# Eight images of an attention-and-convolution layer: four image pairs run as one stream of row bands

## The reference, cut to what matters

```python
stk = _neighborhood(x)                      # [B,H,W,9,C], zero padded
q = einsum('bhwd,de->bhwe', x, Q_P)
k = einsum('bhwkd,de->bhwke', stk, K_P)
v = einsum('bhwkd,de->bhwke', stk, V_P)
alpha = softmax(einsum('bhwke,bhwe->bhwk', k, q) * mask, axis=-1)
t = x + einsum('bhwk,bhwke->bhwe', alpha, v)
t_in = t
t = relu(conv(t, ff1_kernel, ff1_bias))     # 64 -> 64 channels
t = relu(conv(t, ff2_kernel, ff2_bias))     # 64 -> 128
t = relu(conv(t, ff3_kernel, ff3_bias))     # 128 -> 64
return t_in + t
```

## Time and profile before

| | |
|---|---|
| median of 3 runs | 2274.04 us (2273.7 to 2277.18) |
| profiled execution, first to last instruction | 2273.2 us; the trace gives no other time of its own for it |
| mean granted clock of PE | 0.992 of full speed |
| PE busy | 2184.7 us, 96% |
| DVE busy | 1889.0 us, 83% |
| ACT busy | 1133.5 us, 50% |
| share of PE in the chain that ended last | 88% |
| DMA | 328.30 MB, mean 144 GB/s |

### The profile page before, as it was taken

The page is one execution under the profiler, slowest core; times in us unless marked ns, Lnnn a source line. Parts: engine busy times, 40 slices in busy tenths (PEclk is TensorE's granted clock), DMA queues, the critical chain, the costliest instruction groups (busy, mean ns, idle before and its releaser), DMA issues.

```text
span 2273.2 us, 64013 instructions
## 1 busy us (share of the span) xinstructions
PE 2184.7 (96%) x24401; PEld 1227.1 (54%) x24401; DVE 1889.0 (83%) x2850; ACT 1133.5 (50%) x3108; POOL 15.5 (1%) x24
## 2 busy tenths in 40 slices
PE   4999999999899999999989999999998999999998
PEld 2655555555455555555555555555545555555554
DVE  4788888888588888888858888888876888888886
ACT  2554555455355555455435555554535555545542
POOL 2000000000000000000000000000000000000000
PEclk9999999999999999999999999999999999999999
DMA  5445544544255445444535454445443544454453
GB/s 131 135 136 159 155 144 132 172 145 143 96 165 155 145 132 171 145 144 142 162 104 152 133 171 145 144 142 165 144 140 103 169 146 142 142 166 144 135 158 124
DMA packets 291252, 328.30 MB, mean 144 GB/s; under 512 B 89300, under 2 KB 223252, under 8 KB 284564
## 3 DMA queue, kind: packets, MB, share of 16 engines
q1 hardware_dynamic: 291164, 327.17, 47.8%
HBM read 152.50 MB, written 33.82 MB: 82 GB/s over the span
## 4 chain that ended last, share of the span: by engine, by line
PE 88%; DVE 6%; issue 3%; ACT 1%; DMA 1%; SPq 1%; DVEq 0%; ACTq 0%
PE conv_banks L485 30%; PE conv_banks L501 25%; PE conv_banks L443 17%; PE mix_bank L421 6%; PE score_banks L394 4%; DVE work L868 3%; PE score_banks L406 3%; PE mix_bank L433 3%; PE score_banks L386 1%; DMA work<-w 1%; ACT probt L646 0%; DVE prob L767 0%; PE mix_bank L370 0%; ACT prob L629 0%; DVE negmax L758 0%
## 5 line engine op out<-in xcount | busy, mean ns | idle before, releaser
L485 PE MATMUL conv_banks<-dodd,w3f 128*64 128x512 f32 (+1 forms) x1656 | 501.9, 580 | 10.8 <-DVE work L835 8.6
L485 PE MATMUL conv_banks<-deven,w3f 128*64 128x512 f32 (+1 forms) x1656 | 495.6, 569 | 8.7 <-DVE prob L767 7.0
L629 ACT ACTIVATE prob<-score_banks,negmax 128x100 f32<-128x100 f32 x1040 | 343.2, 342 | 189.3 <-DVE negmax L758 189.3
L443 PE MATMUL conv_banks<-dt,w1f 128*64 128x256 f32 (+3 forms) x4224 | 413.5, 383 | 12.3 <-DVE work L868 5.6
L501 PE MATMUL conv_banks<-duh,w2h 64*128 64x512 f32 (+2 forms) x1632 | 327.8, 399 | 3.7 <-DVE work L859 2.6
L443 PEld LDWEIGHTS conv_banks<-dt,w1f 128*64 128x64 f32 (+1 forms) x4224 | 218.9, 135 | 206.2 <-issue 69.5
L501 PE MATMUL conv_banks<-duh,w2l 64*128 64x512 f32 (+2 forms) x1632 | 318.5, 388 | 2.1 <-DVE prob L767 2.1
L501 PE MATMUL conv_banks<-dul,w2h 64*128 64x512 f32 (+2 forms) x1632 | 282.6, 397 | 0.0
L485 PEld LDWEIGHTS conv_banks<-dodd,w3f 128*64 128x64 f32 x1656 | 138.6, 137 | 236.8 <-issue 213.2
L646 ACT COPY probt<-score_banks 100x1024 f32<-100x1024 f32 x130 | 131.7, 1013 | 235.1 <-PE score_banks L406 235.1
L485 PEld LDWEIGHTS conv_banks<-deven,w3f 128*64 128x64 f32 x1656 | 155.6, 138 | 157.2 <-issue 111.4
(11 more groups left out here) (93 smaller groups left out, 2943.7 us busy)
## 6 DMA issues: line engine op xcount, KB each, us to landing
xk<-x_keys SPq DMA_DIRECT2D x66, 800.0 KB
xc<-x_bands SPq DMA_DIRECT2D x66, 650.0 KB, 4.9
dodd<-dodd SPq DMA_DIRECT2D x68, 512.0 KB, 5.1
xr<-x_bands SPq DMA_DIRECT2D x264, 128.0 KB, 3.3
out<-work SPq DMA_DIRECT2D x60, 512.0 KB, 2.6
dt<-dt SPq DMA_DIRECT2D x68, 256.0 KB, 2.3
deven<-deven SPq DMA_DIRECT2D x68, 256.0 KB, 5.5
duh<-duh SPq DMA_DIRECT2D x68, 256.0 KB, 2.4
```

The lines of the kernel that those rows point to most:

```text
L443: mm = nc.tensor.matmul(bank[(LOWER, UPPER)[o], n * 256 + lo * 64:n * 256 + hi * 64], w1f[i][rows, m, s, o * C:o * C + C], dt[rows, lo + s ...
L485: return nc.tensor.matmul(bank[rows, lo * 128:hi * 128], w3f[:, m, s, odd * C:odd * C + C], source[:, lo + s // 2:hi + s // 2, m], start=s ...
L629: last = nc.scalar.activation(prob[:, g % 2, a], score_banks[:, g % 2, a * KEYS:(a + 1) * KEYS], ACT.Exp, bias=negmax[:, g % 2, a:a + 1], ...
```

## The change

The four pairs become one stream of 64 bands. The draining step after each of the first three pairs is gone: the next pair's step 0 is now a whole step in every convolution, and it finishes the old pair's last slot of convolutions 1 and 2 and four slots of convolution 3. Step 1 does four slots of convolution 3 too: two of the old pair and two of the new one. There is one draining step at the end (`DRAIN`) and the same final piece (`LAST`, `FINAL`).

Rows of one pair must not reach into the other. So at k = 0 the half-row taps of convolution 1 start at slot 1, and two taps of convolution 2 are cut at the border: one becomes two matmuls of 1 and 2 slots, one runs over 3 slots in place of 4. At k = 1 two of the six taps of each convolution 3 tile are cut in two matmuls (2 and 1 slots, and 1 and 2). The order of two taps in `conv3_tile` and of the two slots in `begin2` is turned, so that the first matmul on a bank covers all of it.

The order of loops changes: step 0 of the first pair stands ahead of the loop; the loop has three turns of step 1, the inner loop, and the next pair's step 0; the last pair's step 1 and inner loop stand behind it, and then the draining step. `store` has no work in the first step; at k = 1 it writes two pieces of two slots to two places. ACT's copies of zeros and the separate regions at k = 0 go; POOL sets four more buffers to zero at the start.

```diff
 def pairs1(k):
-    return (0, 1) if k == BANDS else (0, RP)
+    return (0, 1) if k == DRAIN else (0, RP)
 def pairs2(k):
-    return (1, RP) if k == 0 else (0, 1) if k == BANDS else (0, RP)
+    return (0, 1) if k == DRAIN else (0, RP)
 def pairs3(k):
-    return (2, RP) if k == 1 else (0, 2) if k == 0 else (0, RP)
+    return (0, 2) if k == LAST else (0, RP)
...
         def schedule(eng, step):
-            with eng.Fori(0, PAIRS) as p:
-                g0, b0 = p * STEPS, p * BANDS
-                step(g0, 0, b0 + 1, 1, True)
-                step(g0 + 1, 1, b0 + 2, 0, True)
+            def pair(p):
+                g0 = p * BANDS
+                step(g0 + 1, p, 1, g0 + 2, 0, True)
                 with eng.Fori(0, (BANDS - 2) // 2) as h:
                     for j in range(2):
-                        step(g0 + h * 2 + (2 + j), 2 + j, b0 + h * 2 + (3 + j), 1 - j, True)
-                step(g0 + BANDS, BANDS, b0 + BANDS, 0, False)
+                        step(g0 + h * 2 + (2 + j), p, 2 + j, g0 + h * 2 + (3 + j), 1 - j, True)
+
+            step(0, None, 0, 1, 1, True)
+            with eng.Fori(0, PAIRS - 1) as p:
+                pair(p)
+                step(p * BANDS + BANDS, p, 0, p * BANDS + (BANDS + 1), 1, True)
+            pair(PAIRS - 1)
+            step(RUN, PAIRS - 1, DRAIN, RUN, 0, False)
...
+            def store(G, p, k):
                 lo, hi = pairs3(k)
                 sp.wait_ge(out_ready, G + 1)
-                sp.dma_start(out[:, G, lo:hi], sums[CONV3][:, lo:hi]).then_inc(sent, 16)
+                first = (G + p) * RP
+                if k == 1:
+                    to = slots[:, bass.ds(first - RP, 12)].rearrange("c (n s) i w -> c n s i w", s=6)[:, :, 0:2]
+                    sp.dma_start(to, sums[CONV3].rearrange("c (n s) i w -> c n s i w", n=2)).then_inc(sent, 16)
+                else:
+                    sp.dma_start(slots[:, bass.ds(first, hi - lo)], sums[CONV3][:, lo:hi]).then_inc(sent, 16)
...
             def tap1(k, i, m, n, rows, o, s, start, stop):
                 lo, hi = pairs1(k)
-                if k == 0 and s == 0:
+                if k == 0 and rows is not FULL:
                     lo = 1
...
                     for i, rows, o in ((0, LOWER, 0), (0, UPPER, 1), (1, UPPER, 0), (1, LOWER, 1)):
-                        if o == 0 and k == 0:
-                            tap1(k, i, m, n, FULL, o, 0, False, n == 1)
-                        elif o == 1 or k < BANDS:
-                            tap1(k, i, m, n, rows, o, 1 - o, n == 0 and k == BANDS, n == 1)
+                        if o == 1 or k != DRAIN:
+                            tap1(k, i, m, n, rows, o, 1 - o, n == 0 and k == DRAIN, n == 1)
...
                 def tap(odd, s, start, stop):
                     rows, source = (LOWER, UPPER)[odd], (dodd, deven)[s % 2]
-                    return nc.tensor.matmul(bank[rows, lo * 128:hi * 128], w3f[:, m, s, odd * C:odd * C + C],
-                                            source[:, lo + s // 2:hi + s // 2, m], start=start, stop=stop)
+                    spans = [(lo, hi)]
+                    if k == 1 and s in (0, 3):
+                        spans = [(0, 2), (3, RP)] if s == 0 else [(0, 1), (2, RP)]
+                    for lo_, hi_ in spans:
+                        mm = nc.tensor.matmul(bank[rows, lo_ * 128:hi_ * 128], w3f[:, m, s, odd * C:odd * C + C],
+                                              source[:, lo_ + s // 2:hi_ + s // 2, m], start=start,
+                                              stop=stop and hi_ == hi)
+                    return mm
...
             def tap2(k, which, j, rows, s, w, d, start, stop):
                 lo, hi = pairs2(k)
+                spans = [(lo, hi)]
+                if k == 0 and (which, rows) == (EVEN, LOWER) and s == 0:
+                    spans = [(0, 1), (2, RP)]
+                if k == 0 and (which, rows) == (ODD, UPPER) and s == 1:
+                    spans = [(1, RP)]
...
-            with pe.Fori(0, PAIRS) as p:
-                g0, b0 = p * STEPS, p * BANDS
-                step(g0, 0, b0 + 1, True)
-                step(g0 + 1, 1, b0 + 2, True)
+            def pair(g0):
+                step(g0 + 1, 1, g0 + 2, True)
                 with pe.Fori(0, BANDS - 2) as h:
-                    step(g0 + h + 2, 2, b0 + h + 3, True)
-                step(g0 + BANDS, BANDS, b0 + BANDS, False)
+                    step(g0 + h + 2, 2, g0 + h + 3, True)
+
+            step(0, 0, 1, True)
+            with pe.Fori(0, PAIRS - 1) as p:
+                pair(p * BANDS)
+                step(p * BANDS + BANDS, 0, p * BANDS + (BANDS + 1), True)
+            pair(RUN - BANDS)
+            step(RUN, DRAIN, RUN, False)
...
+            nc.gpsimd.memset(kept[:, 0], 0.0)
             nc.gpsimd.memset(kept[:, 1, 0:2], 0.0)
+            for t in (dt[:, 0:1], duh[:, 0:1].bitcast(F32), dul[:, 0:1].bitcast(F32)):
+                nc.gpsimd.memset(t, 0.0)
```

More of the change, by code:

```diff
@@ L30 @@
 LOADS = PAIRS * BANDS + 3
+RUN = PAIRS * BANDS
+FINAL = RUN + 1
+DRAIN, LAST = BANDS, BANDS + 1
 NEG = -3.0e38
@@ L70, in new_slots @@
 def new_slots(which, k):
-    return {CONV1: 1, ODD: 1, EVEN: 2}[which] if k == BANDS else RP
+    return {CONV1: 1, ODD: 1, EVEN: 2}[which] if k == DRAIN else RP
 def build(nc, x_bands, x_keys, qt2, kt, vbd, w1, w2, w3, b1, b2, b3, window, eye, eye16, out):
@@ L310, in _, with step @@
             keep_first(1, 0)
-            def store(G, k):
+            slots = out.rearrange("c g s i w -> c (g s) i w")
+            def store(G, p, k):
                 lo, hi = pairs3(k)
                 sp.wait_ge(out_ready, G + 1)
-                sp.dma_start(out[:, G, lo:hi], sums[CONV3][:, lo:hi]).then_inc(sent, 16)
-            def step(G, k, b, par, att):
+                first = (G + p) * RP
[4 more added lines that the diff above has]
+                    sp.dma_start(slots[:, bass.ds(first, hi - lo)], sums[CONV3][:, lo:hi]).then_inc(sent, 16)
+            def step(G, p, k, b, par, att):
                 sp.wait_ge(conv1_done, G * 8 + 8)
@@ L326, in step @@
                 sp.dma_start(deven[:, 0:1], deven[:, RP:RP + 1]).then_inc(v_kept, 16)
-                store(G, k)
+                if p is not None:
+                    store(G, p, k)
                 if att:
@@ L341, in _ @@
             schedule(sp, step)
[L342 to L348, removed]
+            store(FINAL, PAIRS - 1, LAST)
+            sp.wait_ge(sent, 16 * (FINAL + 2))
+            sp.wait_ge(t_kept, 16 * (FINAL + 1))
+            sp.wait_ge(u_kept, 32 * (FINAL + 1))
+            sp.wait_ge(v_kept, 32 * FINAL)
+            sp.wait_ge(carried, 48 * (1 + 2 * RUN))
             sp.wait_ge(xk_in, 16 * (LOADS - 1))
@@ L500, in tap2 @@
                 lo, hi = pairs2(k)
-                return nc.tensor.matmul(conv_banks[:, bank_of(which, j), lo * 128:hi * 128],
-                                        w[rows, STREAMS[j], 2 * (which == EVEN) + s],
-                                        d[rows, lo + s:hi + s, STREAMS[j]], start=start, stop=stop)
+                spans = [(lo, hi)]
[3 more added lines that the diff above has]
+                    spans = [(1, RP)]
+                for lo, hi in spans:
+                    mm = nc.tensor.matmul(conv_banks[:, bank_of(which, j), lo * 128:hi * 128],
+                                          w[rows, STREAMS[j], 2 * (which == EVEN) + s],
+                                          d[rows, lo + s:hi + s, STREAMS[j]], start=start, stop=stop)
+                return mm
             def begin2(G, k, j, ahead=None):
@@ L671, in relu_conv1 @@
                 to = relued[CONV1]
-                regions = [(FULL, lo, hi)]
-                if k == 0:
-                    regions = [(FULL, 1, RP), (UPPER, 0, 1)]
-                if k == BANDS:
-                    regions = [(LOWER, 0, 1)]
-                if k in (0, BANDS):
-                    outside = LOWER if k == 0 else UPPER
-                    nc.scalar.copy(to[outside, 0, :, 1:1 + W], zeros[outside, 0])
-                for rows, lo, hi in regions:
-                    last = nc.scalar.activation(
-                        to[rows, lo:hi, :, 1:1 + W].rearrange("c s i (w n) -> c n s i w", n=2),
-                        sums1[rows, :, lo:hi], ACT.Relu, bias=bias[rows, 0:1])
-                last.then_inc(relu_done, 1)
+                rows = LOWER if k == DRAIN else FULL
+                if k == DRAIN:
+                    nc.scalar.copy(to[UPPER, 0, :, 1:1 + W], zeros[UPPER, 0])
+                nc.scalar.activation(
+                    to[rows, lo:hi, :, 1:1 + W].rearrange("c s i (w n) -> c n s i w", n=2),
+                    sums1[rows, :, lo:hi], ACT.Relu, bias=bias[rows, 0:1]).then_inc(relu_done, 1)
             def relu_conv2(G, k, which, behind=0):
@@ L690, in relu_conv2 @@
                 to = relued[which]
-                if k == 0:
-                    nc.scalar.copy(to[:, 0, :, 1:1 + W], zeros[:, 0])
-                if k == BANDS and which == EVEN:
```

(25 more changed lines are left out.)

54 lines of the change are left out of this document (27 added, 27 removed).

## The result

The changed kernel takes 2203.45 us (median of 4 runs, 2202.78 to 2205.71) against 2273.87 for the kernel before (4 runs, 2271.76 to 2277.18). The ratio is 0.9689 [0.9678, 0.9701]. The forecast was 2211; the kernel is 7.6 us faster than that and inside the range. The profiled execution has a span of 2201.5 us, the forecast one of 2210.3: 8.8 us are to be accounted for.

The account below looks back on a forecast made before the run. PE was taken to bound the inner steps, with standstills at pair borders. Terms of -82.4 (draining steps), +3.1 (first pair) and +16.4 (pairs 2 to 4) summed to -62.9: span 2210.3, time 2211 us, range 2196 to 2221.

Parts of the forecast that it names:

- Three draining steps go, -82.4: Draining steps after the first three pairs vanish, jump back and gap included: 27.26, 27.40 and 27.76 us, -82.4 us together.
- Steps 0 and 1 at 32.94 each: Each pair's first two steps become whole steps on PE, 65.9 us together, bounds -1 and +2 us for a pair.
- The rival in which cut taps break the overlap: Cut taps of convolutions 2 and 3 cost 0.08 us more per matmul: 2233 or 2249 us; chance 0.09.
- the cold start: First pair's steps 0 and 1 cost 2.8 us over warm ones, before and after: 68.7 us, +3.1.
- The jumps, two times 6.47: PE's loop over pairs jumps back twice, each 4.49 us gap plus 1.98 us clock loss: 12.9 us.
- The rival without a gap: PE has no gap at the new jump back of the loop over pairs: 2198 us; chance 0.13.
- DVE's gap covered by PE's longer one: DVE's 2.07 us gap at its jump hides under PE's; uncovered, it would cost 1.5 us each, 3 in all.
- ACT, which I set at nothing: ACT loses some copies of zeros and is busy half of the time; no effect on the span was counted.
- The rival in which DVE's nine written-out steps no longer stay at hand: Each of DVE's 24 inner-loop jumps has the 2.07 us gap, 1.5 reaching PE: 36 us, 2247 us; chance 0.04.
- The end, as before: The last draining step and the final piece keep their time: 70.55 us from the last inner step's mark.
- The other side: Rival: PE's inner loop pays 6.47 us at each of 52 jumps, +336, 2547 us; chance 0.02 with anything as large.
- The signs: In the new trace: 65 marks, later pairs' steps 0 and 1 at 32 to 34 us, two 4-5 us gaps, half clock.

Follow-up runs that it names:

- the kernel before written out: Kernel before the change with the loop over the pairs written out for every engine; 2252.81 us, ratio 0.9902.
- the written-out version: Changed kernel with the loop over the pairs written out, inner loops kept: 2192.88 us for PE alone, 2192.24 us for every engine.

## Why the prediction was right

**Three draining steps go, -82.4.** Right. Less its three gaps (5.13 + 4.39 + 3.94 = 13.5) the term is 68.9, and in the kernel before written out the draining steps take 21.5, 23.6 and 23.6 us over the 32.94 of the inner step, 68.7 together (the granted clock over the three is 1.00, 0.93 and 0.90). Steps 0 and 1, which become fuller, take 7.6 us of that back over the four pairs: 1.8 in the first, and 195.0 against 189.1 us at the three borders, both written out. That leaves 61.1 us by these marks and 60.6 by the medians, which is what one stream is worth by itself.

**Steps 0 and 1 at 32.94 each.** Right, slightly too dear: 32.87 and 32.34. The timeline of PE in the changed kernel, convolution 1 in step 0, convolution 3's first tile in step 1, and the draining step's convolution 3:

```profile
581.64 2.76 PE L460 MATMUL conv_banks<-dt,w1f 128*64 128x256 f32 x32
...
584.82 1.50 PE L505 MATMUL conv_banks<-dodd,w3f 128*64 128x512 f32 x5 [0.43 <-DVE work L860]
...
1682.24 0.49 PE L505 MATMUL conv_banks<-dodd,w3f 128*64 128x256 f32 x2
...
2172.17 1.50 PE L505 MATMUL conv_banks<-dodd,w3f 128*64 128x512 f32 x5 [1.87 <-DVE work L860]
```

The 5.54-us pass of the earlier trace rows is 2.76 us, shorter even than an inner step's 2.97: its half-row taps are narrower. PE then waits 0.43 us for DVE before convolution 3, a small wait that the forecast didn't have and that eats part of it. In step 1 the forecast set 1.1 us for 16 more matmuls against 1.1 us for narrower ones. The net is -0.5 us, which the version without the cuts confirms; that it is the extra matmuls which cost less than 1.1, and not the narrower ones which save more, no run tells apart. The rival in which cut taps break the overlap is refuted. Only the third border's two steps lie clear of a jump and of the start: 65.21 us against 65.9. For the first pair, 67.15 against 68.7, the cold start was put too high as well: 1.9 us over the third border and not 2.8. It differs between executions: in the kernel before written out it is 64.45 - 62.75 = 1.7 us.

**The jumps, two times 6.47.** Right that there are two, that PE's body is too long for the jump to be free, and that the clock falls behind them; the size was off. The gaps are 3.72 and 3.55 us, in place of 4.49. By the borders the jump and its clock cost 70.44 - 65.21 = 5.2 and 71.12 - 65.21 = 5.9 us, by the written-out version 5.6. The gaps of one and the same loop differ: 5.13, 4.39 and 3.94 us in the kernel before, 3.66, 3.30 and 4.17 in the version of it with convolution 1 in groups. So a mean of three was a weak source, and that 3.72 and 3.55 lie below it need not come of the change. Border by border the kernel before pays 6.3 us for a jump all told, close to the forecast's 6.47. The rival without a gap is refuted at two jumps of two.

**DVE's gap covered by PE's longer one.** Right in the sum for a wrong reason, and so by luck. DVE has no gap at the new jump, so there was nothing to cover, and the 3 us that I kept for it in the range had no object. The converse, which I hadn't seen, is what the kernel before with PE written out showed: ACT, which I set at nothing, had a gap of 3.31 us there too. The rival in which DVE's nine written-out steps no longer stay at hand is refuted: neither the outer nor an inner jump of DVE has a gap. That it is the shorter body of the loop which took the outer gap away is argued, from PE's versions with longer bodies and from the packets of q14; no run changed the body of ACT's or DVE's loop alone.

**The end, as before.** 2.8 us shorter, and not by the change. The granted clock was 0.95 over the last 35.0 us, while before, the last 37.6 us had 0.86. The same five matmuls took 1.50 us at 2172.17; in the changed kernel with PE written out, the same code shows, in its timeline of PE:

```profile
2161.47 2.82 PE L505 MATMUL conv_banks<-dodd,w3f 128*64 128x512 f32 x5 [1.33 <-DVE work L860]
```

One profiled execution has the draining step at one clock level and another at the other. A forecast against one span carries some 3 us of that.

**The other side.** PE's inner loop was not touched and paid nothing. The experiment with three steps in its body shows that the rival was real: 12 inner jumps eat more than the whole gain.

**The signs.** Two gaps stand where they were said to, none at the third border, and the clock is low behind them. Two signs were off in size: the gaps are under 4 us, and step 1 behind the second jump takes 1179.29 - 1144.66 = 34.63 us and not 34 at most. And one could not show anything as it was put: the marks number 65 in both kernels, since a draining step has no such product.

## What to carry to other kernels

Count what stands in the body of a loop, for each engine. A body short enough jumps back for nothing; one that is too long costs here some 5 to 8 us a turn on PE, of which about a third is the clock behind the gap, and other engines may hide gaps of their own under PE's. So find out with every engine's loop written out, not with one.

A step that only drains is worth giving up for full steps even when these need cut tiles: here a step with 16 extra matmuls and fewer columns was 0.5 us shorter than a whole one.

Keep taps on full rows together and taps on half rows together: here the order alone cost 1.5 us in a pass of 32 matmuls.

## What the runs showed of the hardware that was not expected

- After the gap at a jump a second one can follow, some 3 us later: 1.06 us at 222.63 in the version with three steps in the inner body, and one behind nine of its 12 inner jumps.
- ACT and DVE have a gap of their own at a jump over five written-out steps (3.31 and 2.00 us), and none that shows over four.
- One loop's gaps differ in size from turn to turn, 3.30 to 5.13 us at the three borders of the kernel before and of its version in groups.
- The low clock behind a wait is not of one length: a wait of 3.00 us was followed by 12.2 us at 0.58, a gap of 5.13 us by 6.2 us at 0.63.
- The fetches are little as transfers: 220 packets in place of 43 take 0.7% of the DMA engines' time, and yet the kernel is 90.5 us slower. The price is that PE stands still meanwhile, and that the granted clock is low behind it, 0.50 over six us at 219.30.
